# Layer 1's last chunk taken in two halves by node

## What is computed

```python
h = relu(layernorm(x))
x = x + relu(segment_sum((h * clip(deg, 1)**-0.5)[src], dst)) @ W.T + b      # layer 0, deg: edges out of a node
h = relu(layernorm(x))
msg = h[src] @ W_msg.T + b_msg + edge_embed[edge_type]
m = segment_sum(msg, dst)
x = x + gru_cell(m, h, W_ih, W_hh, b_ih, b_hh)                           # layer 1
```

```python
r = sigmoid(i_r + h_r);  z = sigmoid(i_z + h_z)
n = tanh(i_n + r * h_n)
return (1 - z) * n + z * h
```

## Time and profile before

| | us |
|---|---|
| median of 3 runs | 918.85 |
| lowest, highest | 918.78, 919.85 |
| profiled execution, its own time | 920.79 |
| its span, first to last instruction | 918.8 |

### The profile page before, as it was taken

How to read it: one execution, slowest core, us unless ns; L and a number is a source line. 1 busy time by engine, 2 the same in 40 slices (tenths; PEclk the granted TensorE clock), 3 DMA queues, 4 the chain that set the end, 5 groups by cost and what they waited for, 6 DMA issues and landing times.

```text
span 918.8 us, 21032 instructions
## 1 busy us (share of the span) xinstructions
PE 845.8 (92%) x8962; PEld 755.5 (82%) x8962; DVE 772.6 (84%) x1044; ACT 502.3 (55%) x924; POOL 96.9 (11%) x77
## 2 busy tenths in 40 slices
PE   2353899999999999999999999999999999999996
PEld 2242788889888888988889988989889888988985
DVE  5898999999999999999999991568766766766876
ACT  1579588888888888888888884211111111111011
POOL 6880203003020030100000000000000000000000
PEclk9995899999999999999999999999999999999998
DMA  3642434336444344543335510497667667667750
GB/s 89 136 142 74 166 145 168 153 151 236 195 179 167 152 172 195 211 181 147 152 146 212 211 34 13 156 299 267 236 272 283 226 248 299 236 233 290 260 211 20
DMA packets 38332, 169.17 MB, mean 184 GB/s; under 512 B 8132, under 2 KB 21387, under 8 KB 35288
## 3 DMA queue, kind: packets, MB, share of 16 engines
q1 hardware_dynamic: 31898, 159.98, 46.2%
q0 software_dynamic: 6000, 6.48, 2.9%
q10 hardware_dynamic: 334, 1.29, 0.5%
HBM read 87.67 MB, written 79.74 MB: 182 GB/s over the span
## 4 chain that ended last, share of the span: by engine, by line
PE 52%; DVE 31%; issue 6%; ACT 5%; POOL 4%; DMA 1%; SPq 0%; DVEq 0%; POOLq 0%; ACTq 0%
PE ps L1323 29%; DVE work L743 11%; DVE work L736 11%; PE ps L1182 9%; PE ps L1171 5%; DVE work L751 4%; POOL tab L494 3%; ACT ring L976 2%; ACT tab L987 1%; PE ps L1275 1%; PE ps L1278 1%; PE ps L1280 1%; PE ps L1276 1%; PE ps L1277 1%; PE ps L1279 1%
## 5 line engine op out<-in xcount | busy, mean ns | idle before, releaser
L1171 PE MATMUL ps<-work 128*128 128x106 f16 x3125 | 431.3, 216 | 46.7 <-ACT ring L976 29.0
L1182 PE MATMUL ps<-ring,tab 125*128 125x250 f16 x2500 | 417.2, 272 | 0.7 <-ACT ring L981 0.7
L976 ACT ACTIVATE ring<-ps 128x848 f16<-128x848 f32 x375 | 330.6, 884 | 75.3 <-PE ps L1171 68.8
L1171 PEld LDWEIGHTS ps<-work 128*128 128x128 f16 x3125 | 286.5, 101 | 70.5 <-ACT ring L976 33.2
L1323 PE MATMUL ps<-ring,tab 125*128 125x250 f16 (+1 forms) x2500 | 277.0, 269 | 0.0
L1323 PEld LDWEIGHTS ps<-ring,tab 125*128 125x128 f16 (+1 forms) x2500 | 242.4, 97 | 28.7
L1182 PEld LDWEIGHTS ps<-ring,tab 125*128 125x128 f16 x2500 | 244.5, 98 | 25.3 <-ACT ring L981 0.9
L736 DVE TENSOR_TENSOR work<-iota_row,mch 128x3906 f16<-128x3906 f16 x100 | 223.4, 2234 | 1.0 <-PE ps L1171 0.5
L743 DVE TENSOR_TENSOR work<-iota_w,mch 128x1550 f16<-128x1550 f16 x200 | 188.1, 981 | 0.0
L824 DVE TENSOR_TENSOR work<-work,ring 125x3250 f16<-125x3250 f16 (+1 forms) x92 | 161.6, 1780 | 0.0
L1119 ACT ACTIVATE tab<-ps,bg 128x250 f32<-128x250 f32 x25 | 11.8, 471 | 147.7 <-PE ps L1276 146.9
(11 more groups left out here) (187 smaller groups left out, 617.3 us busy)
## 6 DMA issues: line engine op xcount, KB each, us to landing
adjacency<-ring SPq DMA_DIRECT2D x23, 2937.5 KB
ring<-adjacency SPq DMA_DIRECT2D x46, 812.5 KB, 6.4
ring<-adjacency SPq DMA_DIRECT2D x46, 750.0 KB, 9.0
adjacency<-ring SPq DMA_DIRECT2D x23, 183.1 KB
out<-x_sb SPq DMA_DIRECT2D x24, 125.0 KB
h_turned<-hst SPq DMA_DIRECT2D x23, 125.0 KB, 2.0
tab<-h_turned SPq DMA_DIRECT2D x23, 125.0 KB, 2.0
x_sb<-x SPq DMA_DIRECT2D x3, 560.0 KB
```

Of the source, the lines that this page charges most:

```text
L976: act.activation(to(x * 2 * u, 2, x), ps[:, s:s + 2, 0:x * SLOTS].rearrange("p b (x h) -> p h b x", h=SLOTS), ACT.Copy).then_inc(sem("evac ...
L1171: last = pe.matmul(ps[:, 2 * (u % 2) + i // BANKW, o:o + WCOLS], lohot[:, s, k, :], combo[:, s, k, :], start=True, stop=True)
L1182: mm = pe.matmul(psD[c % 2], tabv[0][P, h, s, :], adj[c % 2][P, h, :], start=i == 0, stop=i == 2 * BLOCKS - 1)
```

## The change

The last chunk's 100 products of 250 columns become 200 of 125: first all source blocks for block 0 of the pair (columns 0, 2, 4, ... of the adjacency, `j::CB`), then all for block 1, each half in its own bank of `psD`. Each half has its own message, gate products, sigmoids, tanh, state, turn, addition and store, over 125 columns. The old-state products stay 250 wide. TensorE's order is now: half 0 parts 0 and 1; gates of chunk 23; half 0 part 2; old-state products of chunk 24; half 0 part 3; half 1 parts 0 and 1; turn of chunk 23; new gates of half 0; half 1 parts 2 and 3; flag product; turn of half 0; new gates of half 1; turn of half 1. On VectorE the flag follows the state of half 0. Half 0 is stored by SP in one piece, half 1 in two pieces as before.

```diff
-        def last_result(eng, rows):
-            eng.wait_ge(sem("result"), CHUNKS)
-            q = chunk(CHUNKS - 1)
-            eng.dma_start(out_v[rows, blocks(q), :], x_sb[rows, blocks(q), :]).then_inc(sem("out"), 16)
+        def last_result(eng, j, rows):
+            eng.wait_ge(sem("result"), CHUNKS + j)
+            b = CB * chunk(CHUNKS - 1) + j
+            eng.dma_start(out_v[rows, b, :], x_sb[rows, b, :]).then_inc(sem("out"), 16)
...
-            last_result(sp, slice(0, 112))
+            last_result(sp, 0, P)
+            last_result(sp, 1, slice(0, 112))
...
+        def last_gate_vector(v, ch, m, j):
+            n = of_node(j)
+            v.wait_ge(sem("psN"), m + 1 + j)
+            v.wait_ge(sem("r"), m + 1 + j)
+            v.wait_ge(sem("nn"), m)
+            ch.did(v.scalar_tensor_tensor(nin[:, n], psN[:, 1, n], bg_h[:, 2:3], rz[:, 0, n], ALU.add, ALU.mult))
+            ch.wait()
+            v.tensor_tensor(nin[:, n], nin[:, n], psN[:, 0, n], ALU.add).then_inc(sem("nin"), 1)
...
+        def last_out_vector(v, m, j):
+            v.wait_ge(sem("psO"), m + 1 + j)
+            b = CB * chunk(m) + j
+            v.tensor_tensor(x_sb[P, b, :], psO[:, j, :], x_sb[P, b, :], ALU.add).then_inc(sem("result"), 1)
...
-            post1_gate_vector(v, ch, last)
-            v.wait_ge(sem("flag_sum"), 1)
-            v.tensor_scalar(flag_i[:, :], psFlag, 0.0, None, ALU.is_gt).then_inc(sem("flag_set"), 1)
-            last_state_vector(v, ch, last)
-            post1_out_vector(v, last)
+            for j in range(CB):
+                last_gate_vector(v, ch, last, j)
+                last_state_vector(v, ch, last, j)
+                if j == 0:
+                    v.wait_ge(sem("flag_sum"), 1)
+                    v.tensor_scalar(flag_i[:, :], psFlag, 0.0, None, ALU.is_gt).then_inc(sem("flag_set"), 1)
+                last_out_vector(v, last, j)
...
+        def last_chunk_scalar(act, m, j):
+            n = of_node(j)
+            act.wait_ge(sem("used1"), 4 * m + 2 + 2 * j)
+            act.wait_ge(sem("psZ"), m)
+            act.activation(msgs[:, n], psD[(CHUNKS + m + j) % 2][:, 0:LO], ACT.Copy, scale=ginv[:, 0:1])\
+               .then_inc(sem("msg"), 1)
...
+        def last_products_tensor(pe, m, j, part):
+
+            a, b = PARTS[part]
+            for h in range(a, b):
+                K = 128 if h < TB else LO
+                for k in range(2):
+                    last = pe.matmul(psD[(CHUNKS + m + j) % 2][:, 0:LO], tabv[1][0:K, h, k, :],
+                                     adj[slot(m)][0:K, h, j::CB], start=h == 0 and k == 0, stop=h == BLOCKS - 1 and k == 1)
+            if part % 2:
+                last.then_inc(sem("used1"), 1)
+
+        def last_gates_new_tensor(pe, m, j):
+            pe.wait_ge(sem("msg"), m + 1 + j)
+            if j:
+                pe.wait_ge(sem("r"), m + j)
+                pe.wait_ge(sem("nin"), m + j)
+                pe.wait_ge(sem("z"), m + j)
+            n = of_node(j)
...
+        def last_turn_tensor(pe, m, j):
+            pe.wait_ge(sem("hnew"), m + 1 + j)
+            pe.wait_ge(sem("result"), m + j)
+            pe.transpose(psO[:, j, :], hnew[:, of_node(j)], ident[:, :]).then_inc(sem("psO"), 1)
...
-            last_gates_new_tensor(pe, CHUNKS - 1)
+            m = CHUNKS - 1
+            pe.wait_ge(sem("msg"), m - 1)
+            for part in range(4):
+                pe.wait_ge(sem(f"load{slot(m)}_{part}"), 16 * (m // 2))
+                last_products_tensor(pe, m, 0, part)
+                if part == 1:
+                    post1_gates_tensor(pe, m - 1)
+                if part == 2:
+                    last_gates_old_tensor(pe, m)
+            for part in range(4):
+                last_products_tensor(pe, m, 1, part)
+                if part == 1:
+                    post1_turn_tensor(pe, m - 1)
+                    last_gates_new_tensor(pe, m, 0)
             pe.wait_ge(sem("mismatch"), 1)
             pe.matmul(psFlag, over[P, 0:1], ones[P, 0:1], start=True, stop=True).then_inc(sem("flag_sum"), 1)
-            post1_turn_tensor(pe, CHUNKS - 1)
+            last_turn_tensor(pe, m, 0)
+            last_gates_new_tensor(pe, m, 1)
+            last_turn_tensor(pe, m, 1)
```

More of the change, by code:

```diff
@@ L847, in post1_state_vector, with last_state_vector @@
             v.tensor_tensor(hnew, nn, hnew, ALU.add).then_inc(sem("hnew"), 1)
[L849 to L854, removed]
-            ch.wait()
-            v.wait_ge(sem("nn"), m + 1)
-            ch.did(v.tensor_tensor(hnew, new_share, nn, ALU.mult))
-            ch.wait()
-            v.tensor_tensor(hnew, old_part, hnew, ALU.add).then_inc(sem("hnew"), 1)
+        def last_gate_vector(v, ch, m, j):
[4 more added lines that the diff above has]
+            ch.did(v.scalar_tensor_tensor(nin[:, n], psN[:, 1, n], bg_h[:, 2:3], rz[:, 0, n], ALU.add, ALU.mult))
+            ch.wait()
+            v.tensor_tensor(nin[:, n], nin[:, n], psN[:, 0, n], ALU.add).then_inc(sem("nin"), 1)
+        def last_state_vector(v, ch, m, j):
+            n = of_node(j)
+            v.wait_ge(sem("z"), m + 1 + j)
+            v.wait_ge(sem("psO"), m)
+            ch.did(v.tensor_tensor(old_part[:, n], rz[:, 1, n], h1c[:, m % 2, n], ALU.mult))
+            ch.did(v.tensor_scalar(new_share[:, n], rz[:, 1, n], -1.0, 1.0, ALU.mult, ALU.add))
+            ch.wait()
+            v.wait_ge(sem("nn"), m + 1 + j)
+            ch.did(v.tensor_tensor(hnew[:, n], new_share[:, n], nn[:, n], ALU.mult))
+            ch.wait()
+            v.tensor_tensor(hnew[:, n], old_part[:, n], hnew[:, n], ALU.add).then_inc(sem("hnew"), 1)
+        def last_out_vector(v, m, j):
+            v.wait_ge(sem("psO"), m + 1 + j)
+            b = CB * chunk(m) + j
+            v.tensor_tensor(x_sb[P, b, :], psO[:, j, :], x_sb[P, b, :], ALU.add).then_inc(sem("result"), 1)
         def post1_out_vector(v, m):
@@ L1123, in post1_gate_scalar @@
             act.activation(nn, nin, ACT.Tanh, bias=bg_i[:, 2:3]).then_inc(sem("nn"), 1)
+        def last_chunk_scalar(act, m, j):
[4 more added lines that the diff above has]
+               .then_inc(sem("msg"), 1)
+            act.wait_ge(sem("psR"), m + 1 + j)
+            act.wait_ge(sem("hnew"), m)
+            act.activation(rz[:, 0, n], psRZ[0][:, n], ACT.Sigmoid, bias=bg[:, 0:1]).then_inc(sem("r"), 1)
+            act.wait_ge(sem("psZ"), m + 1 + j)
+            act.activation(rz[:, 1, n], psRZ[1][:, n], ACT.Sigmoid, bias=bg[:, 1:2]).then_inc(sem("z"), 1)
+            act.wait_ge(sem("nin"), m + 1 + j)
+            act.activation(nn[:, n], nin[:, n], ACT.Tanh, bias=bg_i[:, 2:3]).then_inc(sem("nn"), 1)
         def scalar_layer1(act):
             post0_scalar(act, CHUNKS - 1)
-            for m in range(CHUNKS):
+            for m in range(CHUNKS - 1):
                 post1_message_scalar(act, m)
                 post1_gate_scalar(act, m)
-            last_result(act, slice(112, LO))
+            for j in range(CB):
+                last_chunk_scalar(act, CHUNKS - 1, j)
+            last_result(act, 1, slice(112, LO))
         def tensor_prepare(pe):
@@ L1285, in last_gates_old_tensor @@
             h = h1c[:, m % 2, :]
-            pe.matmul(psRZ[0], gate_weights(whh_sb, 0), h, start=True, stop=False)
+            pe.matmul(psRZ[0], gate_weights(whh_sb, 0), h, start=True, stop=False, skip_group_check=True)
             pe.matmul(psN[:, 1, :], gate_weights(whh_sb, 2), h, start=True, stop=True)
[L1288 to L1294, removed]
+            pe.matmul(psRZ[1], gate_weights(whh_sb, 1), h, start=True, stop=False, skip_group_check=True)
@@ new lines, in of_node @@
+        def of_node(j):
+            return slice(LO * j, LO * (j + 1))
+        def last_products_tensor(pe, m, j, part):
[7 more added lines that the diff above has]
+                last.then_inc(sem("used1"), 1)
@@ new lines, in last_gates_new_tensor @@
+        def last_gates_new_tensor(pe, m, j):
[4 more added lines that the diff above has]
+                pe.wait_ge(sem("z"), m + j)
+            n = of_node(j)
+            pe.matmul(psRZ[0][:, n], gate_weights(wih_sb, 0), msgs[:, n], start=False, stop=j == CB - 1,
+                      skip_group_check=True).then_inc(sem("psR"), 1)
+            pe.matmul(psN[:, 0, n], gate_weights(wih_sb, 2), msgs[:, n], start=True, stop=True).then_inc(sem("psN"), 1)
+            pe.matmul(psRZ[1][:, n], gate_weights(wih_sb, 1), msgs[:, n], start=False, stop=j == CB - 1,
+                      skip_group_check=True).then_inc(sem("psZ"), 1)
@@ L1330, in tensor_layer1 @@
                         post1_gates_tensor(pe, m - 1)
-                    if m == CHUNKS - 1 and j == 2:
-                        last_gates_old_tensor(pe, m)
                     if m and j == 3:
                         post1_turn_tensor(pe, m - 1)
-            last_gates_new_tensor(pe, CHUNKS - 1)
+            m = CHUNKS - 1
[12 more added lines that the diff above has]
+                    last_gates_new_tensor(pe, m, 0)
```

(8 more changed lines are left out.)

## The result

| us | before | changed |
|---|---|---|
| median of 9 runs each | 919.05 | 921.67 |
| lowest, highest | 918.78, 919.89 | 921.00, 923.27 |
| profiled execution, its own time (span) | 920.79 (918.8) | 921.35 (919.3) |

The ratio is 1.0027, with a 95% interval of 1.0018 to 1.0036: the change costs 2.6 us, between 1.7 and 3.3. The forecast was 920.2, its range 919.0 to 922.6.

A forecast was written before the change was run, and what follows sets the result against it. TensorE, with work in 92% of the span, was taken as the bound. +3.03 us to the last product, -1.52 for the tail and -0.15 for the store gave +1.36, so 920.2 us against 918.85; range 919.0 to 922.6.

The forecast's parts named there:

- slower by over 0.2%: Whole kernel: the case of a time above 920.69 us; chance 0.53.
- the fallen clock: Rival: behind the stall the granted clock falls to 1.2 GHz for 3.4 us, losing 1.7 us, result 921.9; chance 0.25.
- The stall: Last chunk, before the old-state gates: TensorE waits 1.8 us for VectorE's nin of chunk 23, plus 0.1 fill.
- Products: Last chunk: 200 half products at 54.5 ns cost 10.90 us against 10.73 for 100 full ones, +0.17.
- First half's gates and the turn ahead of the last product: TensorE before the last 48 half products: the first half's new gates add 0.72 us, chunk 23's turn 0.22.
- First half's work hidden: First half's gates to state lie under the last 48 products, turn and addition under the second half's work; cost nothing.
- The tail: After the last product: half-width message, gates, VectorE operations and turn save 1.52 us, bounds 1.1 and 1.8.
- The store: Last store after the final addition: half the bytes save 0.15 us, bounds 0 and 0.4.
- 80 ns for short products: Rival: issue or weight loads hold half products at about 80 ns, result 923.3 us; chance 0.10.
- Half rate for the step: Rival: stepped columns read at half rate, 107 ns a half product, result about 929 us; chance 0.04.

The follow-up runs named there:

- taking it away in two ways: Changed kernel with old-state gates after part 0 of the second half's products: ratio 1.0005; or with chunk 23's gate arithmetic ahead of VectorE's second fold: 1.0007 (both against before).
- the kept-busy kernel: Kernel before plus 30 unused products of 125 columns between the flag product and the last turn: 919.50 us, ratio 0.9997 to the kernel before.
- 64 columns: Changed kernel with 64 stepped columns a product instead of 125, leaving out half of the sums: 920.32 us (one execution), kernel before beside it 919.55.
- the 2.36 us stall: Changed kernel with VectorE's third fold also ahead of chunk 23's gate arithmetic: 924.71 us, ratio 1.005 to the kernel before.
- the run with neighbouring columns: Changed kernel with each half's products reading 125 neighbouring adjacency columns instead of every second one: 921.27 us, ratio 1.0018 to the kernel before.
- the gate ahead of the fold: Changed kernel with VectorE's gate arithmetic of chunk 23 ahead of the second fold instead of behind it: 920.12 us, ratio 1.0007 to the kernel before.
- 3.37 and 4.22 us: TensorE waits in two changed-kernel variants: 64 stepped columns a product (920.32 us); third fold and an extra reduction ahead of chunk 23's gate arithmetic (925.91 us).

## Why the prediction was right, and where it was short

The range held the time, and of its cases "slower by over 0.2%" had the most chance. The mechanism was right too: a stall at the old-state gates and small products moved ahead of the last one outweigh the narrower tail. But the forecast itself, +1.36, is about half of the +2.62 between the medians, and the median lies 0.6 us over the forecast's own range of 919.3 to 921.1. That the whole range held it is partly luck: its upper end, 922.6, was there for the fallen clock, and no trace of the changed kernel shows that. By its steps:

**The stall: right in place and cause, too long.** Predicted 1.8 us (bounds 1.7 to 2.0) and 0.1 for filling, at the old-state gates, released by VectorE's second gate operation. Measured 1.33 and 0.18, and 1.51 by taking it away in two ways. It is below its bounds mainly because the 76 products ahead of it ran slower (76 x 4.3 ns = 0.33) and used it up.

**Products: mis-sized.** The step that was off is the choice of 54.5 ns from six products in layer 0. In the changed kernel a product costs 58.8. Of the 4.3 ns, 3 are the step between columns; the other 1.3 separate the long run from a row that could not be read so finely. For the 124 products behind the wait that is +0.53 us. I had bounded it at 52 and 107 ns and chosen the end of the nearest row, which had neighbouring columns. The Trainium skill, SBUF — State Buffer, in its box on cachelines, puts the stride that is free at up to 8 elements of bf16, which is as wide as fp16: the trace does not agree, since a step of 2 costs 58.8 against 55.8 ns.

**First half's gates and the turn ahead of the last product: right.** Predicted 0.72 and 0.22; 0.66 and 0.27 in the chain (three pairs of 0.22, L1360 0.27).

**First half's work hidden: right.** Its state ended at 909.56 in the changed kernel, its turn and addition (910.57 to 911.27) lay under the second half's message and gates, and VectorE was wanted again at 911.95.

**The tail: right, in one term by luck.** Predicted -1.52 with the bounds -1.1 and -1.8; 4.00 - 5.58 = -1.58. The turn gave 0.42 of it (0.81 to 0.39), not the 0.30 that I took for the clock and the missing pass together, and the other terms 1.16 instead of 1.22. I had argued that the turn would meet the higher clock since TensorE is dense until the last product. That doesn't hold: behind products as dense and a wait of 1.91 or 1.92 us, the last turn took 0.39 at the full clock in five of the eight traces of the changed kernel and its variants, 0.48 where the clock fell while it ran, and 0.58 and 0.59 where it fell at its start or before. Which of these an execution gets is open; a fall costs this turn 0.19 us.

**The store: wrong, small.** Predicted -0.15 for half the bytes. From the end of the final addition to the span's end are 4.65 us before and 4.58 with the kept-busy kernel (125 KB); with half the bytes, in the eight traces, from 4.38 to 4.78, mean 4.60. The means differ by 0.02 us, far less than the scatter.

In sum, to the last product's end the traces give (910.52 - 892.24) - (908.57 - 893.86) = +3.57 against 3.03 predicted, nearly all of the difference the 124 products. Less 1.58 that is +1.99, and with the 0.13 by which the two traces differ behind the final addition it is +2.12 against +1.36.

**Rivals.** The fallen clock did not happen in either trace of the changed kernel, and its price was about right (1.62 measured against 1.7). 80 ns for short products fell altogether: 55.8 ns over a run of 76 products, 31.7 at 64 columns. The Trainium skill, TensorE: Matmul & The Clock Gate, section Back-to-back issue gap, gives 81 ns for a sustained stream of load and 128-column product; the trace does not agree. The same section's formula for the isolated gap (N / 2.4 + 2.5) comes nearer, also in a run: 54.6 and 106.7 ns by it for 125 and 250 columns, an estimate from the page, against 55.8 and 107.3 measured. Half rate for the step fell: it costs 5 to 6%, not 100%.

**Open:** in its two groups the changed kernel's median stands 0.3 to 0.7 us further above before than its two traces do. The clock falling in some executions would do it, and the two groups at the 2.36 us stall point that way. But neither trace of the changed kernel shows it, both intervals hold the traces' +1.9 to +2.1, and the run with neighbouring columns, whose stall is longer (1.60 us), has no such rest: +1.57 by its median, +1.63 by its trace. So scatter is the likelier answer, and neither is shown.

**Where the gain went.** By the traces, the half-wide tail brought its 1.58 us. It was paid with 1.51 of stall, 0.93 for the first half's gates and for chunk 23's turn, which used to lie behind the last product, 200 x 58.8 ns less 100 x 107.3 ns = 1.03 for the products, and 0.10 because the first pair of a row of gate pairs takes 0.48 instead of 0.43 behind half-width products, twice. Without the stall that is 0.93 + 1.03 + 0.10 - 1.58 = +0.48, just what the trace with the gate ahead of the fold has (20.77 - 20.29). By these traces the split would not have paid even then; the medians (+0.4 and +0.6) can't be told from no change.

## What to carry to other kernels

Splitting the last tile to shorten the tail brings forward every request of the leading engine, so read the other engines' timelines at the new times, not the old ones: here VectorE's folds, harmless before, stood in front of a value that was asked for 3.6 us earlier, counted from the chunk's start. Count what moves ahead of the last product (small products, turns) at full price, and subtract only that from the narrower tail. And since the engine that waits swallows what is slow ahead of its wait, price only the work behind it.

## What the hardware showed beyond expectation

- A moving operand of fp16 with a step of two elements costs 5 to 6%: 58.8 ns for 125 columns against 55.8 for neighbours; 31.7 for 64 stepped ones.
- Fresh weights for each product set no floor above 31.7 ns: 52 products of 64 columns in a row, against 26.7 for the columns alone at 2.4 GHz.
- Behind waits of 1.33 to 2.36 us inside dense work four traces show the clock at its full level. Behind 3.37 and 4.22 us it fell, 0.7 and 0.3 us after work had begun again, and stood at 1.2 GHz for 3.4 us both times.
- Transposes feel the clock: one takes 0.39 us of the chain at the full level and 0.58 at the lower, behind the same wait.
- The time from the last addition to the end (4.4 to 4.8 us) did not visibly depend on whether 62 or 125 KB were stored.
